# Scores of the last five token tiles as a power on GpSimd, one in each of slots 5 to 9, in place of five exponentials on ScalarE in slot 9

## What is computed

```python
x = x + xattn(layernorm(x), ctx, ctx)       # 16 heads of 16, softmax over heads within a token
# routed feed-forward: 8 experts, 256 -> 512 -> 256, the best one for each token
logits = x_red @ wg_n.T
gates = softmax(logits, axis=1)
scores = max(gates, axis=1)
idx = argmax(gates, axis=1)
h = gelu(x @ W1[idx] + b1[idx])
o = (h @ W2[idx] + b2[idx]) * scores[:, None]
x = x + o
```

## Time and profile before

| | |
|---|---|
| median of 3 runs | 339.85 us (339.45 to 339.86) |
| the profiled execution | 339.95 us |
| its span, first to last instruction | 338.2 us, so 1.75 us lie around it |
| PE busy in the span | 317.1 us (94%) |
| DVE busy | 247.3 us (73%) |
| POOL busy | 241.3 us (71%) |
| ACT busy | 186.9 us (55%) |
| granted TensorE clock | full in the whole span (2.4 GHz) |

### The profile page before, as it was taken

One profiled execution on the slowest core, in us unless ns is written; L12 is line 12 of the kernel. 1 busy time (PEld: TensorE's weight loads), 2 busy tenths in 40 slices (PEclk: granted clock), 3 DMA queues, 4 the chain that ended last, 5 costly groups with the idle time before them and its releaser, 6 DMA issues. The chain is left out here.

```text
span 338.2 us, 10882 instructions
## 1 busy us (share of the span) xinstructions
PE 317.1 (94%) x3799; PEld 259.1 (77%) x3799; DVE 247.3 (73%) x707; ACT 186.9 (55%) x486; POOL 241.3 (71%) x380
## 2 busy tenths in 40 slices
PE   7999899999999999989878799998999999999995
PEld 5777678888888888868666588788989878677773
DVE  7545698888888889799888756887776645655652
ACT  1001567787787778867875746667345434324221
POOL 3598689999999999878889767554377764444323
PEclk9999999999999999999999999999999999999999
DMA  6699888999999999998999311241179968899500
GB/s 233 226 283 293 266 247 258 255 254 274 248 282 287 291 315 308 321 322 254 288 332 410 136 48 54 76 142 37 43 252 396 408 234 292 309 343 306 187 24 31
DMA packets 59364, 80.86 MB, mean 239 GB/s; under 512 B 36766, under 2 KB 46127, under 8 KB 59312
## 3 DMA queue, kind: packets, MB, share of 16 engines
q1 hardware_dynamic: 54864, 68.50, 66.3%
q0 software_dynamic: 3664, 10.81, 9.6%
q10 hardware_dynamic: 784, 0.87, 0.7%
HBM read 59.01 MB, written 21.41 MB: 238 GB/s over the span
## 5 line engine op out<-in xcount | busy, mean ns | idle before, releaser
L455 POOL TENSOR_TENSOR x<-ql,mask 128x1024 f32<-128x1024 f32 x32 | 60.6, 1895 | 2.7 <-DVE r L795 0.5
L1390 PE MATMUL bQ<-w,wA 128*128 x224 | 53.8, 383 | 1.8 <-issue 1.2
L1049 ACT ACTIVATE pad<-ql 64x512 f32<-64x512 f32 x64 | 40.0, 624 | 22.4 <-DMA ql<-qkv_scr 22.0
L1390 PEld LDWEIGHTS bQ<-w,wA 128*128 128x128 f32 x224 | 40.4, 190 | 8.3 <-issue 3.8
L547 POOL DMA_INDIRECT r<-row_scr,idg x34 | 36.0, 1058 | 13.9 <-issue 13.6
L517 POOL DMA_INDIRECT out<-r,ids x21 | 21.6, 1031 | 33.3 <-DVE r L959 31.8
L1072 ACT ACTIVATE ax<-bA,mask 128x256 f32<-128x256 f32 x91 | 36.4, 473 | 3.2 <-PE bA L1253 2.9
L1199 PE MATMUL bY<-wD,oT 128*128 128x265 f32 x128 | 34.6, 392 | 1.4 <-ACT oT L1037 1.3
L1145 PE MATMUL bKV<-wA,cp 128*128 128x256 f32 x128 | 33.2, 382 | 1.1 <-POOL cp L440 1.1
L1241 PE MATMUL bQ<-wA,r 128*128 128x265 f32 x128 | 33.9, 387 | 0.3 <-DVE wA L583 0.3
L1142 PE MATMUL bKV<-wA,r 128*128 128x256 f32 x128 | 33.0, 380 | 1.2 <-DMA r<-in_xc 0.8
(11 more groups left out here) (225 smaller groups left out, 701.2 us busy)
## 6 DMA issues: line engine op xcount, KB each, us to landing
qkv_scr<-qkv SPq DMA_DIRECT2D x16, 768.0 KB, 4.8
ql<-qkv_scr SPq DMA_DIRECT2D x32, 384.0 KB, 5.8
r<-in_xc SPq DMA_DIRECT2D x15, 512.0 KB, 6.1
xt<-in_W1b SPq DMA_DIRECT2D x9, 512.0 KB, 5.2
row_scr<-cat SPq DMA_DIRECT2D x32, 133.5 KB, 5.9
w1b<-in_W1b SPq DMA_DIRECT2D x8, 514.0 KB, 7.2
w<-in_W SPq DMA_DIRECT2D x8, 512.0 KB, 6.6
xt<-in_x SPq DMA_DIRECT2D x15, 256.0 KB, 6.2
```

The source lines that it names most:

```text
L455: eng.tensor_tensor(quarter(kx[:, z % 2, :]), spread(ql[z // 2 % 2][:, :, z % 2, 0:HD]), mask_k, ALU.mult).then_inc(S["kx"], 1)
L1049: i_ = eng.activation(pad[n, z % 3, :].rearrange("p (k g h d) -> p k g h d", k=2, g=NG_, h=2) [:, :, :, h, :], ql[z // 2 % 2][n, :, z % 2, ...
L1390: i_ = eng.matmul(down_bank(b)[:, 0:C], hT[b % 2][:, k, :], w2[:, bass.ds(eb * (KH * C) + k * C, C)], start=(k == 0), stop=(k == KH - 1))
```

## The change

ScalarE loses `scalar_scores`. The exponential is written as a power, e to the logit, by GpSimd: `tensor_tensor` with ALU.pow, the base from a new tile `euler` of 128x8 that a memset fills in step 0. Tile 27 comes in slot 5 (step 39), 28 in slot 6, up to 31 in slot 9, each behind GpSimd's gather and scatter of that slot. The five row stores wait for a new semaphore `powed` in place of `score`. In ScalarE's main loop the exception for slot 9 goes; its other instructions keep their order.

```diff
-SCORES_AT = NEXT + 1
+SCORES_AT = NEXT - 3
+EULER = 2.718281828459045
...
+        euler = sb("euler", [P, NE])
...
         def sync_row(eng, g):
             if live(g):
                 eng.wait_ge(S["nb"], g + 1)
-                eng.wait_ge(S["score"], g + 1)
+                if g < HOLD:
+                    eng.wait_ge(S["score"], g + 1)
+                else:
+                    eng.wait_ge(S["powed"], g - HOLD + 1)
...
             eng.memset(one8[:, :], 1.0)
+            eng.memset(euler[:, :], EULER)
...
             if s + 1 == S1:
                 pool_gather(eng, S1)
+            if live(HOLD + s - SCORES_AT) and s >= SCORES_AT:
+                pool_score(eng, HOLD + s - SCORES_AT)
             if 0 <= s - BIAS_AT < MIX:
                 pool_bias(eng, s - BIAS_AT)
+
+        def pool_score(eng, d):
+            if d == HOLD:
+                eng.wait_ge(S["filled"], 3)
+            eng.wait_ge(S["scaled"], d - HOLD + 1)
+            eng.tensor_tensor(cat[d % CR][:, C:C + NE], euler[:, :], gsc[:, d - HOLD, :], ALU.pow
+                              ).then_inc(S["powed"], 1)
...
-        def scalar_scores(eng):
-            eng.wait_ge(S["scaled"], CR)
-            for d in range(HOLD, NT):
-                eng.activation(cat[d % CR][:, C:C + NE], gsc[:, d - HOLD, :], ACT.Exp).then_inc(S["score"], 1)
-                eng.wait_ge(S["score"], d + 1)
-
...
             for s in range(NEXT, NS + LAGSB):
-                if s != SCORES_AT + 1 and not mixed(s - 3):
+                if not mixed(s - 3):
                     scalar_rows(eng, s)
                 scalar_weights(eng, s)
                 if mixed(s - 2):
                     scalar_rows(eng, s + 1)
                 scalar_ffn(eng, s)
-                if s == SCORES_AT:
-                    scalar_rows(eng, s + 1)
-                    scalar_scores(eng)
```

More of the change, by code:

```diff
@@ L87 @@
         "wqs wTq gsq nr2 wide qq kv kvad qad xb kx pad qk mx lsub exp sm rsm norm tr_a axv axs pvo oT wd x2 nb gm gsub "
-        "scaled score st0 va0 va1 ve rs oh cnt rv selr selp selk invmm texp idg ids yo yb bias0 bias1 bias2 bias3 bias4 first0 first1 second0 second1 "
+        "scaled score powed st0 va0 va1 ve rs oh cnt rv selr selp selk invmm texp idg ids yo yb bias0 bias1 bias2 bias3 bias4 first0 first1 second0 second1 "
         "oh_a cnt_a cnt_r rv_a selr_a selp_a selk_a invmm_a texp_a idg_a taken_a "
```

## The result

The change makes the kernel slower: 341.08 us median of 18 executions (339.36 to 342.66) against 339.81 for the kernel before (18, 339.26 to 341.28), ratio 1.0035 with a 95% interval of 1.0021 to 1.0050. The forecast was no change.

The account below looks back on a forecast made before the run. VectorE's routing, then index matmuls, index lists and gather, was taken as the bound. 339.95 - 0.10 + 0.05 + 0 = 339.90, less 0.10 for the profiled execution lying above the median: 339.8 us, no change; range 338.6 to 341.4.

Parts of the forecast that it names:

- ScalarE's slot 9 isn't on the path; VectorE's routing is.: Path claimed: VectorE's routing, index matmuls, index lists, gather; the 4.5 us leaving ScalarE in slots 9 and 10 lie off it.
- The index matmuls begin at most 0.15 us earlier, 0.10 taken.: Slot 11, TensorE: index matmuls can start at 230.88 at the earliest instead of 231.03; gain taken as 0.10 us.
- The memset of `euler`, 0.05.: Start of GpSimd's stream: one more memset, bounds 0 and 0.12 us, cost taken as 0.05 us.
- Five powers of 1.7 us.: GpSimd, slots 5 to 9: 8.5 us more work, covered by slack and waits; cost 0.
- Port contention at 0, as the row with a power is nearer than that with a stream.: VectorE's routing, 206 to 227 us: slowdown from GpSimd's powers between 0 and 1.6 us, taken as 0.
- Rival A: Powers hold VectorE up in slots 7 to 11, slower: 341.4 us, 10%; stronger form, blocked until power ends, 345.4, 4%.
- TensorE regains its 1.23 us in slot 11 and waits with them for `L877`: TensorE's two waits of 0.40 and 0.83 us become waiting for VectorE's selection matrix; about 1.3 us idle, no cost.
- B: GpSimd gets late in slots 8 to 11 because powers take longer, ScalarE waits for gathers: 340.7 us, 3%.

Follow-up runs that it names:

- the run with six fills: The changed kernel with six idle transposes of TensorE ahead of slot 11's first index matmuls: 339.76 us, ratio 0.9993 to the kernel before.
- third chip: The changed kernel repeated unaltered on another, slower chip: 348.06 us, ratio 0.9990 to the kernel before, which took 348.16 us there.
- experiments 2: The changed kernel with table loads and five exponentials put back on ScalarE, writing to a spare tile: 339.76 us, ratio 0.9988 to the kernel before.
- 3: The kernel before without the exponentials of its last five tiles and without powers: 341.61 us, ratio 1.0034 to the kernel before.
- 4: The changed kernel with three idle transposes of TensorE in slot 11's gap: 340.34 us, ratio 1.0007 to the kernel before.
- 6: The changed kernel with W2's matmuls ahead of the first piece of index matmuls in slot 11: 338.67 us, ratio 0.9956 to the kernel before.
- 7: The kernel before with W2's matmuls ahead of the index matmuls in slot 11, without the change: 340.23 us, ratio 0.9997.

## Why the prediction was wrong

Point by point:

- *ScalarE's slot 9 isn't on the path; VectorE's routing is.* Right. Gelu of slot 10 came at 225.37 (forecast 225.4), and TensorE then waited for the selection matrix.
- *The index matmuls begin at most 0.15 us earlier, 0.10 taken.* They began 0.19 us earlier, but not for the reason given. From the end of the selection matrix to the first index matmul it is 0.15 us before (230.88 to 231.03) and 0.14 after (230.70 to 230.84), so the 0.15 was the time that the hand-over takes and not lateness of ScalarE: this term was worth 0.01. The other 0.18 came from VectorE, which was that much earlier with the matrix, mostly by the one small instruction named above; the forecast had no term for it.
- *The memset of `euler`, 0.05.* It added 0.04 us to GpSimd's row of memsets. Right.
- *Five powers of 1.7 us.* 1.70 median. The first moved the scaled logits of step 40 to 209.83 (forecast 209.3; step 40's own small power took 1.14 us instead of 0.72, beside a long copy of VectorE), without harm. Block 8's gather was issued at 214.77 and taken at 217.93, 0.17 us after its forerunner. Blocks 9 to 11 were each waited for by ScalarE, 0.29, 0.75 and 0.90 us, with TensorE's needs later than that. No cost, as forecast, though with less room than forecast.
- *Port contention at 0, as the row with a power is nearer than that with a stream.* Right: in the profiles no VectorE instruction of the routing grew by more than 0.06 us, with the powers of full width around it, and VectorE's whole way there got 0.18 us shorter. Rival A, in both forms, is out: the run with six fills has all its powers and no loss. Its stronger form, VectorE blocked until the power ends, would have shown at 221.99: that instruction has both inputs in SBUF, starts 0.26 us into a power of 1.75 and takes 0.43 us, as it did without one (0.42).
- *"TensorE regains its 1.23 us in slot 11 and waits with them for `L877`", costed at nothing.* **This is the step that failed.** The wait was seen and sized (1.3 forecast, 1.46 found), but idle time was taken to be worth the same wherever it lies. Two pieces with matmuls between them became one, and behind it the granted clock fell to half for 3.4 us, which cost 1.33 us on the path. No rival had it: A and B gave the right sign by the wrong mechanism.
- *What would make it wrong.* "ScalarE waiting for gathers" was named as B's mark and did appear, harmlessly. That row alone would have misled; the durations of equal matmul groups before and after pointed to the cause.

The measured 341.08 lies inside the range of 338.6 to 341.4, but by luck: the upper end was rival A's price, and the cause is one that the range didn't contain.

## What to carry to other kernels

When a change removes a wait of TensorE but another wait stands close behind, add up where its idle time will lie, not only how much it is: here merged idle time made a fall of the clock more frequent. Equal matmul groups that last longer in the profile behind a gap, with PEclk below 1, show such a fall. If such a gap can't be avoided, move ready work into it (here W2 ahead of the index matmuls, 0.44% faster than before) or, failing that, idle transposes. And count over many executions: a single profile would have shown a fall or none by chance, while the mean clock of every execution shows how often it comes.

## What the runs showed of the hardware that was not expected

- A single idle piece of 1.46 us on TensorE was followed by a fall of its clock to 1.2 GHz in the profiles of the changed kernel and of the one without scores, and in the third chip's profile of the changed kernel it wasn't. With 1.13 us it wasn't either, in the one profile there is. Whether a gap costs anything is not settled by its length alone.
- The fall also comes in other places, in some executions of a kernel and not in others: the profiles of experiments 2, 3, 4, 6 and 7 have one in the attention part, four of them within 2.5 us of the end of an idle piece of about 1 us. In the profile of the run with W2 first it came at 181 us; TensorE had been idle for 1.04 us and busy 0.83 us of the 2 before 180. The same piece stands in the kernel before, in whose profile the clock held. Timeline, W2 first and then before:

```profile
179.82 0.44 PE L1262 MATMUL bA<-ident,a 128*128 128x128 f32 x2 [1.04 <-DVE a L642]
179.94 0.44 PE L1253 MATMUL bA<-ident,a 128*128 128x128 f32 x2 [1.03 <-DVE a L627]
```

Windows of the run with W2 first (us, PE busy, PEclk, DMA share, GB/s):

```profile
178.00:180.00 2.00, 0.83 (x34) 1.00 1.02 362
180.00:182.00 2.00, 1.86 (x39) 0.83 1.01 399
182.00:184.00 2.00, 2.00 (x9) 0.50 1.04 419
184.00:186.00 2.00, 2.00 (x39) 0.81 1.04 410
```

- Leaving out two table loads and five exponentials of ScalarE, 4.5 us of its stream, with every other instruction in its old order, made a kernel 0.34% slower.
- GpSimd's part of a scatter, mostly about 1.0 us, took 2.0 us in slots 11 and 12 of the kernel before (at 229.77 and 234.80), each time begun within 0.11 us of the start of VectorE's 128x2048 instruction of 1.22 us. In the changed kernel the one begun 0.27 us ahead of that instruction took 1.01 us, the one begun 0.10 us into the next took 1.99.
